# Layer 2 of a fused four-layer graph network: norm, turn and routing logits made tile by tile in the second pass

## The chip, the cores and the metric

The kernel runs on 1 core of one Trainium2 chip. The metric is the device time of one execution in microseconds (us), the median of the runs shown.

## What is computed

Four layers stand in a row. Each is a residual step with a graph operator (`gnn`) and a residual step with a feed-forward part (`ffn`), both behind a LayerNorm. There are 3125 nodes with 256 features in float32 and 50000 edges. The change lies where layer 2's graph operator ends and its mixture of experts begins:

```python
# x = x + L2_gnn(layernorm(x), edges, edge_weight, ...)
def _block(x, ei, ew, g, bln, W, b):
    return x + relu(gcn_conv(layer_norm(x, g, bln), ei, ew, W, b))
x = _block(x, ..., ln6_g, ln6_b, W6, b6)
x = _block(x, ..., ln7_g, ln7_b, W7, b7)
return x @ Wp.T + bp

# x = x + L2_ffn(layernorm(x), ...)
shared = relu(relu(x @ sW1 + sb1) @ sW2 + sb2) @ sW3 + sb3
gates = softmax(x @ gW + gb)                 # 4 experts
topv, topi = top_k(gates, 2); topw = softmax(topv)
return shared + sum over the two chosen experts of topw * expert(x)
```

## The kernel before

The nodes stand in T = 25 tiles of P = 125 rows. `X` (the residual) and `XN` (the normed input) lie in SBUF as 25 tiles of 125x256 and stay there from layer to layer. The work is a chain of stages: the context manager `stage` (L83) closes a stage by letting SyncE, ScalarE, TensorE and VectorE drain, add one to `phase_done` and wait until all four have. GpSimd isn't part of these and runs along.

**Layer 2's graph operator** (`layer2_gnn`, L1674). The weighted adjacency matrix lies in DRAM as 25 stripes (`weight_cells`). A pass over the graph takes the 25 stripes one after the other. For each, SyncE loads a block of 125x3125 into one of three buffers (L1716), and TensorE adds up 25 products 125x125 times 125x256 into one PSUM accumulator (L1752, "a block" below; each product is two matmul records in the trace, so 50). There are two passes, `p` = 0 and 1, hence blocks i = 0 to 49. Behind block j TensorE turns tile j-1 (two transposes, L1728) and multiplies tile j-2 by W7 or Wp (L1737), so a pass has T + 2 steps. ScalarE copies what was turned out of PSUM (L1776, L1779). VectorE makes `u` of a block (L1796, L1802); in pass 0 it also norms it (L1806 to L1814, with the root on ScalarE, L1767), in pass 1 it adds bp and the residual for tile j-2 (L1819, L1821). That last add makes the final X of the tile. Beside it all GpSimd scatters edge records for layer 3 (`sort.scatter`, L1669), paced by the blocks.

**Layer 2's mixture** (`layer2_ffn`, L2270) begins with four short stages. The first has SyncE issue 13 loads of the mixture's weights and biases (L2296 to L2301) and waits for none of them. The second is `gate` (L1969), a call of `linear` (L250) with a norm: VectorE takes statistics of all 25 tiles of X (L187) and small terms of all tiles at once (L190 to L204), then scales 13 tiles to `XN` (L208) while ScalarE scales 12 (L218). TensorE turns each tile (L316, two transposes) and two tiles later multiplies it by the 256x4 gate weights (L328), ScalarE copies what was turned (L351), and VectorE adds the bias and puts the logits away (L1972). The third stage is `route` (L1911: softmax, the two best, their weights), the fourth makes the coefficients (L2309, L2312). Then comes the main stage of the mixture: it first waits for the 13 loads, VectorE adds the shared bias sb3 to all of X at once (L2401), and TensorE runs the shared network and the four experts on `XN`, five tiles at a time (L2337, L2355, L2367), while VectorE adds the products to X (L2411, L2413).

Of the kernel before, what the change touches and what calls it, by code (L numbers as in the profile page):

```python
# [1673 lines left out]
def layer2_gnn(nc, g, a, sort):  # L1674
# [4 lines left out]
    with ExitStack() as ctx:  # L1679
# [13 lines left out]
        acc, psT, psL = ps("acc", [128, 3, 512]), ps("psT", [128, 2, 512]), ps("psL", [128, 2, 512])  # L1693
        loaded = [sem(f"loaded{j}") for j in range(BLOCKS)]
# [6 lines left out]
        def _(sp):  # L1701
# [19 lines left out]
        def _(pe):  # L1721
# [20 lines left out]
            for p in range(2):  # L1742
                if p == 1:
                    pe.wait_ge(made_read, T)
                for j in range(T + 2):
                    if j < T:
                        i = p * T + j
                        pe.wait_ge(loaded[i % BLOCKS], 16 * (i // BLOCKS + 1))
                        if i >= 3:
                            pe.wait_ge(acc_read, i - 2)  # L1750
                        for t in range(T):
                            last = nc.tensor.matmul(acc[0:P, i % 3, 0:D], blocks[0:P, i % BLOCKS, t * P:(t + 1) * P],  # L1752
                                                    H[p][0:P, t, :], start=(t == 0), stop=(t == T - 1))
                        last.then_inc(summed, 1)
                    if 1 <= j <= T:
                        turn(p, j - 1)
                    if 2 <= j:
                        multiply(p, j - 2)

        @block.scalar  # L1760
        def _(act):
            act.wait_ge(w_loaded, 16 * 7)
            for p in range(2):
                for j in range(T + 2):
# [16 lines left out]
                    if p == 0 and j >= 2:  # L1781
# [3 lines left out]
                                             scale=g.dinv2[0:P, m:m + 1]).then_inc(made_read, 1)  # L1785

        @block.vector
        def _(dve):
            dve.wait_ge(w_loaded, 16 * 7)
            for p in range(2):  # L1790
                for j in range(T + 2):
# [24 lines left out]
                    if p == 1 and j >= 2:  # L1816
# [5 lines left out]
                        dve.drain()  # L1822

# [145 lines left out]
def gate(nc, g, tag, w, b, n, out, more_loads=()):  # L1969
# [3 lines left out]
    linear(nc, g, tag, g.XN, D, w, b, n, put, norm_of=g.X, more_loads=more_loads)  # L1973

# [295 lines left out]
def layer2_ffn(nc, g, a):  # L2270
# [3 lines left out]
    with ExitStack() as ctx:  # L2274
        sb, ps, sem = bufs(nc, ctx, "f2")
        logits, chosen, weight = sb("logits", [128, T, NE]), sb("chosen", [128, T, 2]), sb("weight", [128, T, 2])
        hot, coef = sb("hot", [128, T, 2, NE]), sb("coef", [128, T, NE])
        s1, s2, s3 = sb("s1", [128, K2, 256]), sb("s2", [128, 2, 128]), sb("s3", [128, D])
        e1, e2, e3 = sb("e1", [128, K2, NE, H1]), sb("e2", [128, NE, H2]), sb("e3", [H2 + 1, NE, D])
        sb1_, sb2_, sb3_ = sb("sb1", [128, 2]), sb("sb2", [128, 1]), sb("sb3", [128, D])  # L2280
        eb1, eb2 = sb("eb1", [128, NE]), sb("eb2", [H2, NE])
        loaded = sem("loaded")

        with stage(nc, g) as block:
            @block.sync
            def _(sp):
                for out, src in ((s1[:, :, :], a["L2_ffn_sW1"].rearrange("(k p) n -> p k n", p=128)),
                                 (s2[:, :, :], a["L2_ffn_sW2"].rearrange("(k p) n -> p k n", p=128)),
                                 (s3[:, :], a["L2_ffn_sW3"]),
                                 (e1[:, 0], a["L2_ffn_eW1"][:, 0:128, :].rearrange("e p n -> p e n")),  # L2290
                                 (e1[:, 1], a["L2_ffn_eW1"][:, 128:256, :].rearrange("e p n -> p e n")),
                                 (e2[:, :, :], a["L2_ffn_eW2"].rearrange("e p n -> p e n")),
                                 (e3[0:H2], a["L2_ffn_eW3"].rearrange("e p n -> p e n")),
                                 (e3[H2:H2 + 1, :, :], a["L2_ffn_eb3"].rearrange("(a e) n -> a e n", a=1)),
                                 (sb3_[:, :], a["L2_ffn_sb3"].partition_broadcast(128))):
                    sp.dma_start(out, src).then_inc(loaded, 16)  # L2296
                with nc.allow_non_contiguous_dma("a few hundred values"):
                    sp.dma_start(sb1_[:, :], a["L2_ffn_sb1"].rearrange("(k p) -> p k", p=128)).then_inc(loaded, 16)
                    sp.dma_start(sb2_[:, :], a["L2_ffn_sb2"].rearrange("(p k) -> p k", k=1)).then_inc(loaded, 16)
                    sp.dma_start(eb1[:, :], a["L2_ffn_eb1"].rearrange("e p -> p e")).then_inc(loaded, 16)  # L2300
                    sp.dma_start(eb2[:, :], a["L2_ffn_eb2"].rearrange("e p -> p e")).then_inc(loaded, 16)  # L2301

        gate(nc, g, "f2g", a["L2_ffn_gW"], a["L2_ffn_gb"], NE, logits)
# [23 lines left out]
        def _(pe):  # L2327
            pe.wait_ge(loaded, 208)
# [43 lines left out]
        def _(act):  # L2372
            act.wait_ge(loaded, 208)
# [321 lines left out]
def build(nc, a, out):  # L2695
    with ExitStack() as ctx:
# [60 lines left out]
        with ExitStack() as sorted_edges:  # L2757
            g.slots = sorted_edges.enter_context(nc.sbuf_tensor("slots", [128, ST + R // 2, 4], F32))
            with ExitStack() as keep:
# [7 lines left out]
                layer2_gnn(nc, g, a, sort)  # L2767
                layer2_ffn(nc, g, a)
# [24 lines left out]
```

## Time and profile before

| | |
|---|---|
| median of 3 runs | 4196.51 us (4194.24 to 4197.27) |
| the profiled execution | 4226.76 us |
| its span | 4225.0 us |
| mean granted TensorE clock | 0.864 |
| TensorE busy | 3233.1 us (77%) |
| VectorE busy | 1454.5 us (34%) |
| ScalarE busy | 809.9 us (19%) |
| GpSimd busy | 2336.8 us (55%) |

Busy times and all rows are those of the one profiled execution. Times within it are us from the start of its span. "PEld" is TensorE's weight load, which overlaps its matmuls; "PEclk" is the TensorE clock that was granted, as a share of 2.4 GHz. "issue" stands for time in which an engine waited for nothing that the profile shows, "remote" for a release that the profile doesn't place on an engine.

### The profile page before, as it was taken

The page shows a single profiled execution, that of the slowest core. Times are in us where ns is not written, and L with a number is a line of the kernel's source. Part 1 is how long each engine was busy: PE and PEld are TensorE (multiplying, and loading weights), DVE is VectorE, ACT ScalarE, POOL GpSimd, SP SyncE. Part 2 cuts the span into 40 slices and gives each one's busy share as a digit, 9 for nine tenths or more (in the row PEclk, how much of TensorE's full clock was granted, in tenths as well). Part 3 has the DMA queues.
Part 4 walks back from the last instruction along what each step waited for, and adds up shares of the span by engine and source line. Part 5 has one row for each costly group of instructions (what it writes and reads, how often), then busy time and mean ns, then how long its engine had stood idle before and what let it go on. Part 6 is the DMA issues. An engine that isn't in the chain of part 4 may idle for free.

```text
span 4225.0 us, 52499 instructions
## 1 busy us (share of the span) xinstructions
PE 3233.1 (77%) x18065; PEld 2470.3 (58%) x18066; DVE 1454.5 (34%) x3546; ACT 809.9 (19%) x2103; POOL 2336.8 (55%) x1876
## 2 busy tenths in 40 slices
PE   0899965485999997699189999969879555555698
PEld 0555553364999997588178878855534333333565
DVE  3333345623461113311721111133343343444344
ACT  0666631211000001133221000013310000001111
POOL 5587888887666666566646656510000666664121
PEclk9999986777999997699599999979989666776799
DMA  8664222124999997487434333400034433335432
GB/s 335 244 187 111 5 6 6 1 18 88 297 282 285 260 264 181 111 227 228 88 132 137 125 123 123 138 16 0 0 126 139 138 92 91 94 91 126 124 114 78
DMA packets 345581, 552.26 MB, mean 131 GB/s; under 512 B 175479, under 2 KB 221473, under 8 KB 328435
## 3 DMA queue, kind: packets, MB, share of 16 engines
q1 hardware_dynamic: 180208, 377.11, 27.8%
q0 software_dynamic: 161552, 132.29, 16.3%
q10 hardware_dynamic: 3600, 40.00, 2.3%
q8 instruction: 128, 2.10, 0.2%
q14 instruction: 93, 0.76, 0.1%
HBM read 410.96 MB, written 137.73 MB: 130 GB/s over the span
## 4 chain that ended last, share of the span: by engine, by line
PE 52%; POOL 19%; issue 13%; DMA 5%; DVE 4%; ACT 1%; ACTq 1%; SPq 1%; another core or an unknown queue 1%; DVEq 1%; POOLq 0%; PEldq 0%
POOL count_cells L465 15%; PE g_acc L1752 13%; PE g_acc L1438 13%; PE g3g_pp L942 5%; PE g_psO L1878 4%; POOL g3g_got L929 3%; PE f3e_pH L2636 3%; PE f_pR L2355 3%; PE f3e_pY L2645 2%; DMA count_cells<-cells_count,added_row 1%; PE f1e_pH L2166 1%; PE f1e_pY L2188 1%; DMA g3g_got<-relations,g3g_idx 1%; POOL weight_cells L882 1%
## 5 line engine op out<-in xcount | busy, mean ns | idle before, releaser
L882 POOL DMA_INDIRECT weight_cells<-added_weight,added_row x391 | 632.0, 1616 | 286.5 <-DMA weight_cells<-added_weight,added_row 158.4
L929 POOL DMA_INDIRECT g3g_got<-relations,g3g_idx x416 | 402.4, 967 | 699.9 <-ACTq L95 509.7
L465 POOL DMA_INDIRECT count_cells<-cells_count,added_row x391 | 651.6, 1666 | 209.6 <-issue 118.6
L1438 PE MATMUL g_acc<-XN,g_blocks 125*125 125x128 f32 x5000 | 565.0, 274 | 42.4 <-DMA g_blocks<-count_cells 40.0
L1752 PE MATMUL g_acc<-g_H,g_blocks 125*125 125x256 f32 x2500 | 562.4, 383 | 30.9 <-issue 16.1
L1438 PEld LDWEIGHTS g_acc<-XN,g_blocks 125*125 125x125 f32 x5000 | 556.8, 189 | 47.1 <-issue 40.2
L942 PE MATMUL g3g_pp<-g3g_got,g3g_hot 128*125 128x256 f32 x832 | 333.1, 543 | 275.0 <-issue 205.2
L1752 PEld LDWEIGHTS g_acc<-g_H,g_blocks 125*125 125x125 f32 x2500 | 473.8, 190 | 112.5 <-issue 40.8
L1669 POOL DMA_INDIRECT slots_dram<-sort_rec,sort_row x392 | 379.5, 968 | 274.2 <-issue 110.2
L942 PEld LDWEIGHTS g3g_pp<-g3g_got,g3g_hot 128*125 128x125 f32 x832 | 192.9, 259 | 415.3 <-issue 234.6
L968 DVE TENSOR_TENSOR X<-X,g3g_pp 125x256 f32 x416 | 175.3, 421 | 347.3 <-DMA edges_other<-digits_dram 179.8
L735 ACT ACTIVATE same_same<-same_scores 128x128 bf16<-128x128 f32 (+7 forms) x392 | 255.1, 651 | 145.4 <-PE same_scores L724 127.9
L720 PE MATMUL same_scores<-edges_other,edges_own 11*128 11x512 bf16 (+2 forms) x490 | 206.9, 483 | 22.5 <-ACT same_same L735 22.5
L1796 DVE SCALAR_TENSOR_TENSOR g_tmp<-g_acc,dinv,g_b 125x256 f32<-125x256 f32 x50 | 24.2, 484 | 517.0 <-PE g_acc L1752 334.9
L1878 PE MATMUL g_psO<-g_w,g_xT 128*125 128x512 f32 x400 | 174.5, 597 | 0.0
L1459 ACT ACTIVATE g_uT<-g_psT 128x125 f32<-128x125 f32 (+1 forms) x75 | 20.6, 275 | 612.0 <-PE g_psT L1413 475.8
L2613 POOL DMA_INDIRECT out_x<-f3e_ys,f_to x32 | 31.2, 976 | 189.9 <-DVE f3e_ys L2691 189.9
L2166 PEld LDWEIGHTS f1e_pH<-f1e_xT,f1e_w 128*128 128x128 f32 x1040 | 125.9, 194 | 16.6 <-ACT f1e_xT L2197 8.7
L2166 PE MATMUL f1e_pH<-f1e_xT,f1e_w 128*128 128x128 f32 x1040 | 130.2, 279 | 6.6 <-ACT f1e_xT L2197 4.4
L1878 PEld LDWEIGHTS g_psO<-g_w,g_xT 128*125 128x125 f32 x400 | 75.6, 190 | 95.3 <-issue 95.1
L722 PE MATMUL same_scores<-edges_other,edges_own 11*128 11x128 bf16 x392 | 119.9, 306 | 7.7 <-DMA edges_other<-digits_dram 7.7
L2188 PE MATMUL f1e_pY<-w,f1e_hT 128*128 x512 | 122.0, 381 | 0.0
(647 smaller groups left out, 4713.0 us busy)
## 6 DMA issues: line engine op xcount, KB each, us to landing
g_blocks<-count_cells SPq DMA_DIRECT2D x500, 312.5 KB
g_blocks<-weight_cells SPq DMA_DIRECT2D x50, 1562.5 KB
count_cells<-edges_stripe ACTq DMA_DIRECT2D x25, 1562.5 KB
weight_cells<-edges_stripe POOLq DMA_DIRECT2D x25, 1562.5 KB
f1e_w<-in_L_ffn_w SPq DMA_DIRECT2D x68, 512.0 KB
relations<-g_ys SPq DMA_DIRECT2D x25, 896.0 KB
f_w<-in_L_ffn_w SPq DMA_DIRECT2D x16, 1024.0 KB
f1e_b<-in_L_ffn_b SPq DMA_DIRECT2D x68, 128.0 KB
```

Of the source, the lines that this page charges most:

```text
L465: pool.indirect_dma_start(out=rows, out_offset=bass.IndirectOffsetOnAxis(ap=g.cell_row[:, t:t + 1], axis=0), in_=g.cell_count[:, t:t + 1], ...
L720: nc.tensor.matmul(self.scores[:, k % self.SCORES, lo:hi], own[:, j, n:n + 128], other[:, j, lo:hi], start=True, stop=True)
L735: self.nc.scalar.activation(self.same[:, k % self.SAME, 0:n], self.scores[:, k % self.SCORES, 0:n], ACT.Relu, accum_out=self.found[:, k:k ...
L882: pool.indirect_dma_start(out=rows, out_offset=bass.IndirectOffsetOnAxis(ap=g.cell_row[:, t:t + 1], axis=0), in_=g.cell_weight[:, t:t + 1] ...
L929: pool.indirect_dma_start(out=got[:, j, :], out_offset=None, in_=table[:, :], in_offset=bass.IndirectOffsetOnAxis(ap=idx[:, n:n + 1], axis ...
L942: last = nc.tensor.matmul(pp[0:P, n // 2 % BANKS, half], hot[:, j, :], got[:, j, :], start=True, stop=True)
L968: last = nc.vector.tensor_tensor(part, part, pp[0:P, n // 2 % BANKS, half], ALU.add)
L1438: last = nc.tensor.matmul(acc[0:P, i % ACCS, 0:128], blocks[0:P, i % BLOCKS, t * P:(t + 1) * P], rhs[p][:, t, :], start=(t == 0), stop=(t ...
L1669: pool.indirect_dma_start(out=g.slots_dram[:, :], out_offset=bass.IndirectOffsetOnAxis(ap=self.row[:, c:c + 1], axis=0), in_=self.rec[:, c ...
L1752: last = nc.tensor.matmul(acc[0:P, i % 3, 0:D], blocks[0:P, i % BLOCKS, t * P:(t + 1) * P], H[p][0:P, t, :], start=(t == 0), stop=(t == T ...
L1878: last = nc.tensor.matmul(psO[0:P, c, :], xT[:, j, k, :], w[:, k, 2 * c:2 * c + 2, :].rearrange("p r n -> p (r n)"), start=(k == 0), stop= ...
L2166: last = nc.tensor.matmul(pH[:, j % 2, f * 128:(f + 1) * 128], w1[:, j % AHEAD, k, f * 128:(f + 1) * 128], xT[:, j % 2, k * 128:(k + 1) * ...
```

## The change

The stages of loads and of the gate are taken out of `layer2_ffn`. What they did is done in pass 1 of `layer2_gnn`, by two new classes.

`TileGate` holds the gate's work for one tile: `norm` (VectorE: statistics, a small sum, then the scaling to `XN`), `root` (ScalarE), `turn` (TensorE, two transposes into a PSUM bank of its own), `copy` (ScalarE), `multiply` (TensorE, four columns into the same bank) and `put` (VectorE). There is one buffer of each, and the turn of tile t waits for the norm of t and for the put of t-1. In step j of pass 1, VectorE norms tile j-2 as soon as its X is done, and puts tile j-3; TensorE turns tile j-3 in the middle of block j and multiplies it at the end of the step. The pass gets one step more, T + 3.

`SharedExperts` holds the mixture's weights. SyncE issues the gate's two loads and the 13 loads of the mixture just ahead of the load of block 25, that is of pass 1's first. Behind the norm of a tile VectorE adds the shared bias sb3 to that tile of X; the add over all of X in the main stage goes, as do that stage's three waits for the loads.

```diff
@@ layer2_gnn, SyncE @@
                 if i == 0:
                     sp.wait_ge(g.weights_added, 16 * (EC + 1))
+                if i == T:
+                    gating.load(sp)
+                    loads.load(sp)
@@ TensorE @@
-                for j in range(T + 2):
+                for j in range(T + 2 + p):
                     if j < T:
...
                         for t in range(T):
+                            if p == 1 and t == T // 2 and j >= 3:
+                                gating.turn(pe, j - 3)
                             last = nc.tensor.matmul(acc[0:P, i % 3, 0:D], blocks[0:P, i % BLOCKS, t * P:(t + 1) * P],
...
                     if 1 <= j <= T:
                         turn(p, j - 1)
-                    if 2 <= j:
+                    if 2 <= j < T + 2:
                         multiply(p, j - 2)
+                    if p == 1 and j >= 3:
+                        if j >= T:
+                            gating.turn(pe, j - 3)
+                        gating.multiply(pe, j - 3)
@@ ScalarE @@
+                    if p == 1 and j >= 3:
+                        gating.copy(act, j - 3)
...
+                    if p == 1 and 2 <= j < T + 2:
+                        gating.root(act, j - 2)
@@ VectorE @@
                         nc.vector.tensor_tensor(g.X[0:P, j - 2, :], tmp2[0:P, :], g.X[0:P, j - 2, :], ALU.add)
                         dve.drain()
+                        gating.norm(dve, j - 2)
+                        if j == 2:
+                            dve.wait_ge(loads.loaded, 208)
+                        nc.vector.tensor_tensor(g.X[0:P, j - 2, :], g.X[0:P, j - 2, :], loads.sb3[0:P, :], ALU.add)
+                    if p == 1 and j >= 3:
+                        gating.put(dve, j - 3)
@@ class TileGate @@
+    def norm(self, dve, t):
+        nc, x = self.nc, self.g.X[0:P, t, :]
+        nc.vector.bn_stats(self.st[0:P, :], x)
+        dve.drain()
+        nc.vector.bn_aggr(self.mv[0:P, :], self.st[0:P, :])
+        dve.drain()
+        nc.vector.tensor_scalar(self.ve[0:P, :], self.mv[0:P, 1:2], EPS, None, ALU.add).then_inc(self.var_ready, 1)
+        dve.wait_ge(self.std_ready, t + 1)
+        nc.vector.reciprocal(self.rstd[0:P, :], self.std[0:P, :])
+        dve.drain()
+        nc.vector.tensor_scalar(self.g.XN[0:P, t, :], x, self.mv[0:P, 0:1], self.rstd[0:P, :],
+                                ALU.subtract, ALU.mult).then_inc(self.normed, 1)
+    def turn(self, pe, t):
+        pe.wait_ge(self.normed, t + 1)
+        if t:
+            pe.wait_ge(self.put_away, t)
+        for k in range(K2):
+            last = nc.tensor.transpose(self.bank[:, k * P:(k + 1) * P], g.XN[0:P, t, k * 128:(k + 1) * 128], g.ident[0:P, 0:P])
+        last.then_inc(self.turned, 1)
+    def copy(self, act, t):
+        act.wait_ge(self.turned, t + 1)
+        if t:
+            act.wait_ge(self.made, t)
+        self.nc.scalar.copy(self.xT[:, :, :], self.bank[:, 0:K2 * P]...).then_inc(self.turn_read, 1)
+    def multiply(self, pe, t):
+        pe.wait_ge(self.turn_read, t + 1)
+        if t == 0:
+            pe.wait_ge(self.loaded, 32)
+        for k in range(K2):
+            last = self.nc.tensor.matmul(self.bank[0:P, 256:256 + self.n], self.xT[:, k, :], self.w[:, k, :], ...)
+        last.then_inc(self.made, 1)
@@ layer2_ffn @@
-        gate(nc, g, "f2g", a["L2_ffn_gW"], a["L2_ffn_gb"], NE, logits)
...
-            pe.wait_ge(loaded, 208)
...
-            act.wait_ge(loaded, 208)
...
-            dve.wait_ge(loaded, 208)
-            nc.vector.tensor_tensor(g.X[0:P], g.X[0:P], wide(sb3_[0:P, :], P, T, D), ALU.add)
```

TensorE at the end of pass 1 and at the start of the gate, before (`g_acc` is a block, `g_psT` and `g_psL` the pass's own turn and multiply, `f2g_psT` and `f2g_psO` the gate's; an f32 matmul here is two records in the trace):

```order
L1752 MATMUL g_acc<-g_H,g_blocks 125x256 x25
L1728 MATMUL g_psT<-ident,g_u 128x125 x2
L1737 MATMUL g_psL<-g_wp,g_uT 125x256 x2
L1728 MATMUL g_psT<-ident,g_u 128x125 x2
L1737 MATMUL g_psL<-g_wp,g_uT 125x256 x4
L99 UNCONDITIONAL_BRANCH x2
L304 UNCONDITIONAL_BRANCH
L316 MATMUL f2g_psT<-ident,XN 128x125 x6
L328 MATMUL f2g_psO<-f2g_w,f2g_xT 125x4 x2
```

The same place now, from the last block on (`g_gate` is the gate's bank: `g_gate<-ident,XN` a turn, `g_gate<-f2g_w,f2g_xT` a multiply):

```order
L1758 MATMUL g_acc<-g_H,g_blocks 125x256 x12
L2038 MATMUL g_gate<-ident,XN 128x125 x2
L1758 MATMUL g_acc<-g_H,g_blocks 125x256 x13
L1732 MATMUL g_psT<-ident,g_u 128x125 x2
L1741 MATMUL g_psL<-g_wp,g_uT 125x256 x2
L2052 MATMUL g_gate<-f2g_w,f2g_xT 125x4 x2
L1732 MATMUL g_psT<-ident,g_u 128x125 x2
L1741 MATMUL g_psL<-g_wp,g_uT 125x256 x2
L2038 MATMUL g_gate<-ident,XN 128x125 x2
L2052 MATMUL g_gate<-f2g_w,f2g_xT 125x4 x2
L1741 MATMUL g_psL<-g_wp,g_uT 125x256 x2
```

Each of blocks 28 to 49 is now split by a turn of the gate, and a multiply of the gate follows each step; behind the last block three tiles of the gate are left, where there were 25.

VectorE in one step of pass 1 now; before, only the first four rows stood there:

```order
L1810 SCALAR_TENSOR_TENSOR g_tmp<-g_acc,dinv,g_b 125x256
L1816 SCALAR_TENSOR_TENSOR g_u<-g_tmp,XN 125x256
L1833 TENSOR_TENSOR g_tmp<-g_psL,g_bp 125x256
L1835 TENSOR_TENSOR X<-g_tmp,X 125x256
L2017 BN_STATS f2g_st<-X 125x6
L2019 BN_AGGR f2g_mv<-f2g_st 125x2
L2021 TENSOR_SCALAR f2g_ve<-f2g_mv 125x1
L2023 RECIPROCAL f2g_rstd<-f2g_std 125x1
L2025 TENSOR_SCALAR XN<-X,f2g_mv,f2g_rstd 125x256
L1840 TENSOR_TENSOR X<-X,f_sb 125x256
L2060 TENSOR_TENSOR f2g_logits<-g_gate,f2g_bias 125x4
```

The last seven rows are new in the step: the norm of the tile whose X was just made, the shared bias, and the put of the tile before it.

## Rows read from the trace of the kernel before

**Rows 1.** The page, the chain that ended last by engine.
```profile
PE 52%; POOL 19%; issue 13%; DMA 5%; DVE 4%; ACT 1%; ACTq 1%; SPq 1%; another core or an unknown queue 1%; DVEq 1%; POOLq 0%; PEldq 0%
```
**Rows 2.** Windows: length, busy us (count) by engine, clock, DMA share, GB/s.
```profile
2467.45:2785.68 318.23, 306.30 (x1386) 259.30 (x1387) 40.55 (x92) 9.88 (x46) 181.63 (x188) 0.98 0.33 113
2785.68:2839.38 53.70, 32.46 (x166) 31.21 (x164) 21.24 (x80) 16.03 (x42) 0.00 (x0) 0.57 0.13 31
```
**Rows 3.** Chain of waits: a clean block, then behind pass 1 (start, us, what).
```profile
2623.41 10.79 PE g_acc L1752 x50
2634.20 0.21 PE g_psT L1728 x2
...
2788.62 0.42 DVE X L1821
...
2789.64 0.43 DVE X L1821
...
2790.32 0.38 SPq L2296
...
2799.21 4.67 DVE f2g_st L187 x14
...
2809.93 1.51 PE f2g_psT L316 x6
2811.44 0.69 PE f2g_psO L328 x4
...
2836.86 2.33 PE f2g_psO L328 x12
2839.22 0.16 DVE f_logits L1972
```
**Rows 4.** Timeline: a clean block of pass 1, and the pass's end.
```profile
2623.24 2.97 PE L1752 MATMUL g_acc<-g_H,g_blocks 125*125 125x256 f32 x13
2623.48 0.42 DVE L1819 TENSOR_TENSOR g_tmp<-g_psL,g_bp 125x256 f32<-125x256 f32 x1
2624.00 0.42 DVE L1821 TENSOR_TENSOR X<-g_tmp,X 125x256 f32<-125x256 f32 x1
...
2787.32 0.42 DVE L1821 TENSOR_TENSOR X<-g_tmp,X 125x256 f32<-125x256 f32 x1
```
**Rows 5.** Timeline: first and last operation of one tile's norm in pass 0.
```profile
2175.03 0.43 DVE L1806 BATCH_NORM_STATS2 g_st<-XN 125x6 f32<-125x256 f32 x1
...
2176.46 0.41 DVE L1814 TENSOR_SCALAR g_u<-XN,g_mv,g_rstd 125x256 f32<-125x256 f32 x1
```
**Rows 6.** Windows of layer 1's table and of the gate, and groups of the first.
```profile
984.00:998.00 14.00, 14.00 (x129) 13.93 (x128) 7.80 (x24) 10.46 (x29) 11.59 (x8) 1.00 0.24 2
2811.10:2836.80 25.70, 25.70 (x136) 25.68 (x134) 6.02 (x31) 13.52 (x34) 0.00 (x0) 0.50 0.00 1
...
L316 PE MATMUL g1a_psT<-ident,XN 125*128 125x125 f32 x42 | 8.0, 272 | 0.0
```
**Rows 7.** Timeline at two late blocks, and who VectorE waited for in pass 1.
```profile
2574.74 10.96 PE L1752 MATMUL g_acc<-g_H,g_blocks 125*125 125x256 f32 x50
2580.95 0.42 DVE L1821 TENSOR_TENSOR X<-g_tmp,X 125x256 f32<-125x256 f32 x1
...
2598.49 3.83 PE L1752 MATMUL g_acc<-g_H,g_blocks 125*125 125x256 f32 x17
2603.27 0.42 DVE L1821 TENSOR_TENSOR X<-g_tmp,X 125x256 f32<-125x256 f32 x1
...
DVE g_tmp L1796 <- PE g_acc L1752: 162.0, 17, 18.1
```
**Rows 8.** Window in which block 25 is loaded.
```profile
2430.70:2437.00 6.30, 6.30 (x32) 5.49 (x31) 2.25 (x7) 1.26 (x4) 4.49 (x5) 1.00 0.76 258
```
**Rows 9.** Timeline: the shared bias, and VectorE's first product in the mixture.
```profile
2850.11 6.83 DVE L2401 TENSOR_TENSOR X<-X,f_sb 125x6400 f32<-125x6400 f32 x1
2870.05 0.42 DVE L2411 TENSOR_TENSOR f_acc<-f_pO,X 125x256 f32<-125x256 f32 x1 [13.11 <-PE f_pO L2367]
```

More of the change, by code:

```diff
@@ L1763, in _ @@
             for p in range(2):
-                for j in range(T + 2):
+                for j in range(T + 2 + p):
+                    if p == 1 and j >= 3:
+                        gating.copy(act, j - 3)
                     if p == 0 and j < T:
@@ L1790, in _ @@
             for p in range(2):
-                for j in range(T + 2):
+                for j in range(T + 2 + p):
                     if j < T:
@@ L2267, in _, with __init__, load, layer2_ffn @@
                         norm.tile_act(t)
-def layer2_ffn(nc, g, a):
+class SharedExperts:
+    def __init__(self, nc, g, a, ctx):
+        NE, _, H1 = a["L2_ffn_eW1"].shape
+        H2 = a["L2_ffn_eW2"].shape[2]
+        sb, ps, sem = bufs(nc, ctx, "f2")
+        self.nc, self.a = nc, a
+        self.s1, self.s2, self.s3 = sb("s1", [128, K2, 256]), sb("s2", [128, 2, 128]), sb("s3", [128, D])
+        self.e1, self.e2, self.e3 = sb("e1", [128, K2, NE, H1]), sb("e2", [128, NE, H2]), sb("e3", [H2 + 1, NE, D])
+        self.sb1, self.sb2, self.sb3 = sb("sb1", [128, 2]), sb("sb2", [128, 1]), sb("sb3", [128, D])
+        self.eb1, self.eb2 = sb("eb1", [128, NE]), sb("eb2", [H2, NE])
+        self.H2 = H2
+        self.loaded = sem("loaded")
+    def load(self, sp):
+        nc, a, H2, loaded = self.nc, self.a, self.H2, self.loaded
+        for out, src in ((self.s1[:, :, :], a["L2_ffn_sW1"].rearrange("(k p) n -> p k n", p=128)),
+                         (self.s2[:, :, :], a["L2_ffn_sW2"].rearrange("(k p) n -> p k n", p=128)),
+                         (self.s3[:, :], a["L2_ffn_sW3"]),
+                         (self.e1[:, 0], a["L2_ffn_eW1"][:, 0:128, :].rearrange("e p n -> p e n")),
+                         (self.e1[:, 1], a["L2_ffn_eW1"][:, 128:256, :].rearrange("e p n -> p e n")),
+                         (self.e2[:, :, :], a["L2_ffn_eW2"].rearrange("e p n -> p e n")),
+                         (self.e3[0:H2], a["L2_ffn_eW3"].rearrange("e p n -> p e n")),
+                         (self.e3[H2:H2 + 1, :, :], a["L2_ffn_eb3"].rearrange("(a e) n -> a e n", a=1)),
+                         (self.sb3[:, :], a["L2_ffn_sb3"].partition_broadcast(128))):
+            sp.dma_start(out, src).then_inc(loaded, 16)
+        with nc.allow_non_contiguous_dma("a few hundred values"):
+            sp.dma_start(self.sb1[:, :], a["L2_ffn_sb1"].rearrange("(k p) -> p k", p=128)).then_inc(loaded, 16)
+            sp.dma_start(self.sb2[:, :], a["L2_ffn_sb2"].rearrange("(p k) -> p k", k=1)).then_inc(loaded, 16)
+            sp.dma_start(self.eb1[:, :], a["L2_ffn_eb1"].rearrange("e p -> p e")).then_inc(loaded, 16)
+            sp.dma_start(self.eb2[:, :], a["L2_ffn_eb2"].rearrange("e p -> p e")).then_inc(loaded, 16)
+def layer2_ffn(nc, g, a, gating, loads):
     NE, _, H1 = a["L2_ffn_eW1"].shape
@@ L2280, in layer2_ffn @@
[L2280 to L2301, printed above, removed]
```

46 lines of the change are left out of this document (38 added, 8 removed).

## The prediction

> **What bounds the kernel now.** I read the page first. The chain that ended last is over half TensorE's [rows 1]. Then the windows of the stretch that the change touches. The second pass of layer 2 runs from 2467.45 to 2785.68 us with TensorE busy for 306.30 of 318.23 us at a clock of 0.98, while VectorE is busy for 40.55 us and ScalarE for 9.88. The stretch from the end of its last block to the last logit takes 53.70 us [rows 2]. So inside the pass each microsecond added to TensorE costs one, and work of VectorE and ScalarE is free as long as TensorE doesn't wait for it; behind the pass everything stands on the chain.
>
> The chain of waits says what those 53.70 us are: the last X is done at 2790.07, SyncE issues fifteen loads until VectorE may begin the statistics at 2799.21, the first tile is turned at 2809.93, TensorE turns and multiplies 25 tiles until 2839.19, and the last logit is done at 2839.38 [rows 3]. Over those 25 tiles the granted clock is 0.50, that is 1.2 of 2.4 GHz [rows 6].
>
> **What goes.** Two stages (loads, gate) and all that stands in them: what is left of the 53.70 us is the new tail.
>
> **The new tail.** VectorE sets it. When the last block ends, three tiles are left. Tile 22's two adds (of bp, and to X) stand where they did and end at 2787.74 [rows 4]; such a pair takes 1.02 us, from 2788.62 to 2789.64 [rows 3]. Behind it now comes the norm. Its price is a row of pass 1, which does the same steps: from the statistics at 2175.03 to the end of the scaling at 2176.87 is 1.84 us [rows 5], 1.92 with the gap ahead. Then the shared bias, an add of 125x256 like the two of a pair, 0.52 with its gap (2623.48 to 2624.00) [rows 4], and the put of the tile before, 0.22 (0.16 in [rows 3] and a gap). So tile 22 is done at 2787.7 + 2.7 = 2790.4, and tiles 23 and 24 follow at 1.02 + 2.66 = 3.68 us each: 2797.7. TensorE's turns and multiplies of 22 and 23 fit between. After the last norm the last tile must still be turned, copied, multiplied and put; in the old gate stage the first tiles took from 2809.93 to 2811.44 + 0.69 = 2812.13 at the low clock [rows 3], 2.2 us, and the put 0.16: 2800.1. The tail is 2800.1 - 2785.7 = 14.4 us in place of 53.7, **39.3 us less**. Routing follows as before.
>
> **What TensorE takes on inside the pass.** Of the 25 tiles, 22 are turned and 21 multiplied ahead of the last block's end; I charge 22. A tile brings two transposes and four matmul records of four columns, each with a weight load: six pairs. In a clean block the two transposes of the pass's own turn cost 0.21 us at the full clock, at 2634.20 [rows 3]. A pair with 128 columns cost 14.00 / 129 = 0.109 us at a clock of 1.00 in layer 1's table, and the same six pairs as here cost 25.70 / 136 = 0.189 us each at 0.50 [rows 6]. I take 0.109 (an estimate: 0.189 halved would be 0.095): 6 x 0.109 = 0.65 us, 22 x 0.65 = **14.3 us more**. Bounds: the narrow matmuls free, 22 x 0.21 = 4.6; all at the low clock's price, 22 x 1.13 = 24.9.
>
> **What TensorE may wait for.** The turn of tile j-3 stands 24 matmul records into block j (24 of 50 records that take 10.79 us [rows 3], 5.2 us) and waits for the norm and for the put behind it. In a clean block the pass's X is done at 2624.42, the norm, the shared bias and the put take 1.92 + 0.52 + 0.22 = 2.66 us more, 2627.08, and TensorE comes to the turn at 2623.24 + 5.2 = 2628.4 [rows 4, 5]: **slack 1.4 us**, no wait. What stands behind the turn on TensorE is the other half of the block, so a miss costs its full length. Three blocks of the pass show a miss to come: there VectorE sees the block's end some 3 us late. In the first X ends at 2581.37, with 2.66 us more at 2584.03, while TensorE began the next block at 2574.74 and comes to the turn at 2579.94: it would wait 4.1 us. In the second it is 2603.69 + 2.66 against 2598.49 + 5.2, so 2.7 us; the third, near 2718, is like the first: 10.9 us in all [rows 7]. The profiled execution is 30 us above the median, so some of this lateness may belong to the profiling; I take half, **5.4 us**, and keep 0 and 10.9 as bounds.
>
> **Edits at nothing.** ScalarE's 25 copies and 25 roots: in the old gate stage it was busy for 13.52 us with the copies and half of the scalings [rows 6], and in the pass it is idle for 97% of 318 us [rows 2]; were it late, the multiply at the block's end, 6 us behind the copy, would wait. SyncE issues the fifteen loads ahead of block 25's: that delays this transfer by some 9 us of issue (2790.32 to 2799.21 [rows 3]) and some 6 us of moving their 1.7 MB (31 GB/s over 53.70 us [rows 2]) at the 258 GB/s of a block's load. Block 25's load moved from 2430.7 to 2437.0 [rows 8], and TensorE used it from 2467.45 [rows 2]; 30 us of slack cover 15. The next block's load waits for a later sum anyway. The wide bias add of 6.83 us in the mixture's stage goes, and it was hidden: VectorE waited 13.11 us for its first product after it [rows 9]. GpSimd's scatter is paced by the blocks, not by this.
>
> **The sum.** -39.3 + 14.3 + 5.4 = -19.6 us. The profiled execution took 4226.8 us (span 4225.0), 30.3 above the median of the runs, and should come to 4207.2, span 4205.4; taken from the median of 4196.5 it is **4176.9 us**.
>
> One thing speaks against this change. The granted clock is 1.00 in clean blocks of the passes [rows 8], though each has two transposes; but it was 0.50 through the whole old gate stage, although TensorE was never idle there [rows 6]. The Trainium skill, "TensorE: Matmul & The Clock Gate", Part 4, says that transposes don't count as TensorE being busy, and that page's part on oscillation warns of short pauses between bursts. By that rule, if the new turns and waits lowered the clock, the time would come out as in rival 2 and not as in the sum; layer 1's table argues against it, since it stood at 1.00 with 42 of 129 matmul records transposes [rows 6]. So the trace agrees only in part.
>
> **Rivals.**
> 1. *The pass gives most of it back.* Narrow pairs at the low clock's price and every late block paid in full: -39.3 + 24.9 + 10.9 = -3.5, 4193.0 us. For it: the one row with four-column matmuls has that price. Against: that row's clock. Chance 0.09.
> 2. *The clock falls inside the pass.* A block's 50 records take 10.79 us at the full clock [rows 3]; at half they take twice that. 22 blocks give 237 us more, 4414 us; it decides against the change from two blocks on. Chance 0.02.
> 3. *VectorE late in every block.* The wait for the norm in the middle of a block replaces the gate stage. With 25.0 us in hand (39.3 - 14.3) and 1.4 us of slack, it turns the sign once VectorE is 25.0 / 22 + 1.4 = 2.5 us later in every block. At the 4.1 us lost in the worst block it is 90 - 25 = 65 us: 4262 us, slower. For it: VectorE gets eleven operations for four, and the slack is small. Against: in 17 blocks of the pass VectorE's first instruction was released by TensorE's block on time [rows 7]. Chance 0.03.
> 4. *It doesn't do what it says:* the loads delay block 25, or routing waits for something else that the gate stage had hidden. At most the 9.1 us of the load stage (2790.07 to 2799.21) come back, 4186 us; nothing in the windows points there. Chance 0.04.
>
> The forecast has 0.82. In it nearly all is faster by more than 8.4 us, 0.2%, which is about what a measurement of this kernel can tell from no change. Rival 4 too is faster; rival 1 is within 0.2%; 2 and 3 are slower. Faster 0.86, same 0.09, slower 0.05. The range runs from the best bounds, -39.3 + 4.6 = -34.7 (4161.8), to rival 1's, a little inside both: 4162 to 4192.
>
> **What the changed profile should show.** The second pass some 20 us longer (338), blocks of 12.5 us instead of 11.87; from the end of the last block to the last logit 14 us; routing starting some 20 us earlier; the old gate stage's lines gone; the granted clock in the pass still near 0.98. Waits of TensorE's new transposes for the scaling on VectorE should be few, and where VectorE sees a block's end late. Many of them, or a clock under 0.9 in the pass, would make the prediction wrong; so would a tail over 25 us.

## The result, and the profile after

| | before | after |
|---|---|---|
| median of 8 runs each | 4195.38 us (4185.87 to 4213.36) | 4173.91 us (4162.06 to 4182.66) |
| ratio, 95% interval | | 0.9944 (0.9930 to 0.9958) |
| the profiled execution, its span | 4226.76, 4225.0 us | 4177.88, 4176.1 us |
| mean granted TensorE clock | 0.864 | 0.874 |

The change is faster by 0.56%, about 23.5 us at the ratio (17.6 to 29.4 over the interval); 19.6 was forecast. The profiled pair lies 48.9 us apart, over twice as much, so it alone can't be read as the effect.

The page of the changed kernel: busy time by engine, and the chain that ended last by engine (before: [rows 1]).

```profile
PE 3210.9 (77%) x18065; PEld 2452.1 (59%) x18066; DVE 1474.7 (35%) x3648; ACT 808.1 (19%) x2115; POOL 2328.0 (56%) x1876
...
PE 51%; POOL 21%; issue 12%; DMA 5%; DVE 5%; ACTq 1%; another core or an unknown queue 1%; ACT 1%; SPq 1%; DVEq 1%; POOLq 0%; PEldq 0%
```

The windows of pass 1 and of what follows it, in the columns of [rows 2].

```profile
2459.00:2782.00 323.00, 316.55 (x1521) 273.19 (x1522) 78.79 (x245) 24.37 (x95) 185.42 (x193) 0.98 0.34 114
2782.00:2798.00 16.00, 8.95 (x40) 6.48 (x38) 9.35 (x33) 4.04 (x12) 0.00 (x0) 0.70 0.00 1
```

VectorE has 245 records in the pass where it had 92, TensorE is busy for 98% of it, and the clock is 0.98 in both kernels. The old stretch of 53.70 us is gone; what follows the pass has 40 TensorE records instead of 166.

The chain of waits of the changed kernel: one clean step of the pass, then the last wait in the pass and the tail (start, us, what).

```profile
2504.06 0.21 PE g_gate L2038 x2
2504.27 5.61 PE g_acc L1758 x26
2509.88 0.21 PE g_psT L1732 x2
2510.10 0.86 PE g_psL L1741 x4
2510.96 0.33 PE g_gate L2052 x4
2511.30 5.28 PE g_acc L1758 x24
...
2523.49 0.33 PE g_gate L2052 x4
...
2782.39 0.21 PE g_psT L1732 x2
...
2792.81 0.41 DVE XN L2025
...
2793.77 0.66 PE g_gate L2038 x2
2794.46 0.38 ACT f2g_xT L2045
2794.88 1.02 PE g_gate L2052 x4
2795.92 0.16 DVE f2g_logits L2060
```

A step is now 12.52 us (2510.96 + 0.33 to 2523.49 + 0.33); before it was 10.79 + 0.21 and the 0.87 of the pass's multiply. The 0.65 us more are the new turn, 0.21, the new multiply, 0.33, and 0.10 in the block itself, whose two parts take 5.28 + 5.61 = 10.89. The last block's end is seen by VectorE at 2782.43 and the last logit is done at 2796.08: a tail of 13.65 us for 53.70.

One step of the pass in the timeline of the changed kernel shows the slack (operation, shapes, and in brackets the idle time before).

```profile
2661.84 0.42 DVE L1835 TENSOR_TENSOR X<-g_tmp,X 125x256 f32<-125x256 f32 x1
...
2663.76 0.41 DVE L2025 TENSOR_SCALAR XN<-X,f2g_mv,f2g_rstd 125x256 f32<-125x256 f32 x1
2664.09 0.42 DVE L1840 TENSOR_TENSOR X<-X,f_sb 125x256 f32<-125x256 f32 x1
2664.42 0.15 DVE L2060 TENSOR_TENSOR f2g_logits<-g_gate,f2g_bias 125x4 f32<-125x4 f32 x1
2666.70 0.38 PE L2038 MATMUL g_gate<-ident,XN 125*128 125x125 f32 x2
```

The put ends at 2664.57 and the turn starts at 2666.70: 2.1 us of slack, where 1.4 were forecast. And the waits of TensorE in the changed kernel's pass (who waited for whom: us in total, times, longest).

```profile
PE g_gate L2038 <- DVE f2g_logits L2060: 5.9, 2, 3.0
```

Only two turns waited, for the put. The timeline of the second one shows why.

```profile
2764.90 0.38 PE L1732 MATMUL g_psT<-ident,g_u 125*128 125x125 f32 x2
...
2770.26 0.48 DVE L1810 SCALAR_TENSOR_TENSOR g_tmp<-g_acc,dinv,g_b 125x256 f32<-125x256 f32 x1 [13.30 <-remote]
2770.30 0.43 ACT L1791 COPY g_uT<-g_psT 128x125 f32<-128x125 f32 x2 [8.91 <-remote]
...
2774.78 0.65 PE L2038 MATMUL g_gate<-ident,XN 125*128 125x125 f32 x2 [3.02 <-DVE f2g_logits L2060]
```

TensorE had ended the block and begun the next turn at 2764.90, yet VectorE's first instruction behind it starts at 2770.26, 5.4 us later, where it is 0.20 in a clean step (2782.23 and 2782.43 at the pass's end). Everything behind it comes late, the put too. VectorE had been idle for 13.30 us, so it is not the added work that made it late, and ScalarE's copy of the turned tile (the turn ends at 2765.28) starts only at 2770.30 as well. What held both up is not shown. The other one, at 2719.79, has the same start: 2710.09 and 2712.85.

### The profile page after: what moved, and what is told of

Same layout as the page of the kernel before. It is cut to its first block, busy times and chain, and to the rows that moved or that the text cites. A ratio compares the mean times of both kernels' runs of the same rounds, so it can differ in the third digit from the quotient of the medians.

```text
span 4176.1 us, 52647 instructions
## 1 busy us (share of the span) xinstructions
PE 3210.9 (77%) x18065; PEld 2452.1 (59%) x18066; DVE 1474.7 (35%) x3648; ACT 808.1 (19%) x2115; POOL 2328.0 (56%) x1876
## 4 chain that ended last, share of the span: by engine, by line
PE 51%; POOL 21%; issue 12%; DMA 5%; DVE 5%; ACTq 1%; another core or an unknown queue 1%; ACT 1%; SPq 1%; DVEq 1%; POOLq 0%; PEldq 0%
POOL count_cells L465 15%; PE g_acc L1438 13%; PE g_acc L1758 12%; POOL g3g_got L929 5%; PE g_psO L1898 4%; PE g3g_pp L942 3%; PE f3e_pH L2732 3%; PE f2m_pR L2454 3%; PE f3e_pY L2741 2%; PE f1e_pH L2254 2%; PE f1e_pY L2276 2%; DMA count_cells<-cells_count,added_row 2%; POOL weight_cells L882 1%; DMA count_cells<-edges_stripe 1%
## 5 line engine op out<-in xcount | busy, mean ns | idle before, releaser
L1438 PE MATMUL g_acc<-XN,g_blocks 125*125 125x128 f32 x5000 | 564.9, 274 | 39.3 <-DMA g_blocks<-count_cells 36.9
L1810 DVE SCALAR_TENSOR_TENSOR g_tmp<-g_acc,dinv,g_b 125x256 f32<-125x256 f32 x50 | 24.2, 484 | 477.4 <-PE g_acc L1758 259.9
L2254 PEld LDWEIGHTS f1e_pH<-f1e_xT,f1e_w 128*128 128x128 f32 x1040 | 125.7, 194 | 12.5 <-ACT f1e_xT L2285 5.2
```

What stands on the lines that cost most here:

```text
L1438: last = nc.tensor.matmul(acc[0:P, i % ACCS, 0:128], blocks[0:P, i % BLOCKS, t * P:(t + 1) * P], rhs[p][:, t, :], start=(t == 0), stop=(t ...
L2254: last = nc.tensor.matmul(pH[:, j % 2, f * 128:(f + 1) * 128], w1[:, j % AHEAD, k, f * 128:(f + 1) * 128], xT[:, j % 2, k * 128:(k + 1) * ...
```

## Experiments

They ran in three batches, on chips that the record numbers 3 (loads moved, turn at 20 and at 3, multiply twice), 5 (changed again, the two with the wide bias add, 128 columns beside) and 10 (before again, the two delays, TensorE warmed up). For the pair above the record names no chip. The kernel before took 4117.7, 4116.7 and 4113.9 us in the three batches, where it took 4195 in the pair above. So it and the changed one were also run again, each with a trace, and the other traces are compared with these two. Each ratio is against the kernel before in the same batch. None leaves work out; some add work whose result is not used.

| kernel | median us | ratio (95%) | pass | tail | main | rest |
|---|---|---|---|---|---|---|
| before, again | 4115.47 | 1.0003 (0.9991 to 1.0015) | 300.1 | 53.80 | 208.9 | 1100.2 |
| changed, again | 4083.24 | 0.9920 (0.9905 to 0.9935) | 314.0 | 14.05 | 202.8 | 1100.5 |
| loads moved alone | 4107.66 | 0.9979 (0.9969 to 0.9988) | 300.1 | 44.92 | 209.6 | 1100.8 |
| turn at product 20 | 4085.45 | 0.9931 (0.9919 to 0.9943) | 314.0 | 14.05 | 202.7 | 1099.8 |
| turn at product 3 | 4131.97 | 1.0034 (1.0021 to 1.0047) | 358.7 | 14.04 | 202.8 | 1100.2 |
| multiply twice | 4095.80 | 0.9947 (0.9933 to 0.9962) | 323.2 | 15.23 | 202.6 | 1099.2 |
| wide bias add back | 4088.64 | 0.9930 (0.9915 to 0.9945) | 314.0 | 13.38 | 207.0 | 1102.8 |
| wide bias, turn at 20 | 4089.34 | 0.9932 (0.9915 to 0.9949) | 314.1 | 13.27 | 204.3 | 1102.1 |
| 128 columns beside, in old gate | 4134.02 | 1.0044 (1.0030 to 1.0058) | 300.1 | 75.08 | 209.7 | 1099.8 |
| main stage 1.4 us later | 4089.15 | 0.9939 (0.9920 to 0.9958) | 314.0 | 14.01 | 202.3 | 1099.2 |
| main stage 2.7 us later | 4088.82 | 0.9941 (0.9921 to 0.9961) | 314.0 | 14.05 | 204.4 | 1096.2 |
| TensorE warmed up | 4087.73 | 0.9930 (0.9909 to 0.9950) | 317.0 | 14.05 | 204.9 | 1099.4 |

The last four columns are read from each kernel's one trace: "pass" from VectorE's first instruction behind block 24 to that behind block 49, "tail" from there to the last logit done, "main" from TensorE's first turn in the mixture's main stage to the start of VectorE's last add of a product to the running sum `acc`, "rest" what follows. Routing and coefficients between tail and main take 11.15 us before and 11.32 after.

### The two kernels again

> The kernel before, profiled beside the next ones. If the stalls and late blocks of the first pair belong to the chip and not to the kernel: 25 blocks of 11.87 us in pass 1, 53.7 us from the last block's end to the last logit, and the mixture's main stage at 203 to 210 us from its first turn to its last product. Rival (they are the kernel's): again some 20 us of stalls in pass 1.

> The changed kernel itself, beside the next ones on the same chip. My sum: 20 us less than before, 0.995. Rival (the 49 us of the profiled pair are the change's own): 0.990 or less.

The changed kernel comes to 0.9920 of the time before, a larger gain than the expected 0.995, and a smaller one than the rival's 0.990. Two kernels that differ from the changed one by almost nothing (the turn at product 20, the first delay) have 0.9931 and 0.9939. So the gain in these batches is some 25 to 33 us.

In both traces every block of pass 1 is clean, which makes them the best reading of the change, though they are of two batches. From the kernel before to the changed one the pass takes 13.9 us more, the tail 39.75 less, routing 0.2 more, the main stage 6.1 less, the rest 0.3 more, and the pass starts 0.8 earlier; together 32.4, the difference of the spans (4114.6 and 4082.2), and close to that of the medians. The windows of the pass show neither kernel idle nor at a low clock, first before, then changed:

```profile
2454.00:2740.00 286.00, 286.00 (x1350) 248.16 (x1349) 40.71 (x92) 9.91 (x46) 180.33 (x187) 1.00 0.37 125
```

```profile
2453.00:2753.00 300.00, 300.00 (x1478) 261.20 (x1478) 79.08 (x245) 22.46 (x90) 182.82 (x189) 1.00 0.36 120
```

So the lateness of VectorE's view of a block, on which the prediction put 5.4 us, is in neither trace. That speaks for the expectation's first reading, that the kernel doesn't cause it. Whether the chip does is not shown.

### The loads alone

In the kernel before, the 13 loads of the mixture's weights go ahead of block 25's, and their stage goes; the gate stays as it was.

```diff
+                if i == T:
+                    loads.load(sp)
@@ layer2_ffn @@
-        with stage(nc, g) as block:
-            @block.sync
-            ...
```

> The kernel before, with the 13 loads of the mixture issued ahead of block 25's load, and the load stage gone. My sum (the tail is worth 39.3 us, of which the load stage is 9.1, and the loads cost nothing in pass 1): 9 us less than the kernel before, the last X to the first statistics 0.2 us in place of 9.1, no wait of TensorE for block 25. Rival (the loads delay block 25 or cost TensorE something in the pass): no change or slower, with a wait of TensorE for g_blocks at the start of pass 1.

The tail falls from 53.80 to 44.92 us and the pass stays at 300.1: the load stage was worth 8.9 us, and the loads in their new place cost nothing. The chain of waits of this kernel behind the pass shows what is left between the last X and the statistics:

```profile
2746.65 0.42 DVE X L1823
...
2747.45 4.67 DVE f2g_st L187 x14
```

From the end of the last X at 2747.08 it is 0.4 us, where it was 9.1 [rows 3]. Of the tail's 39.75 us, 8.9 are the loads', the other 30.9 the gate's.

### Where the turn stands

```diff
-                            if p == 1 and t == T // 2 and j >= 3:
+                            if p == 1 and t == 20 and j >= 3:
```

> The changed kernel with the gate's turn behind the 20th of a block's 25 products instead of the 12th: TensorE comes to it 3.5 us later and has 5.6 us of slack in place of 2.1. My theory (TensorE waits for VectorE in a few blocks only, 5.9 us in the profiled execution): no wait for the gate's turn inside the pass, clean blocks 12.52 us as in the changed kernel, the same tail, 2 to 6 us less. Rival (the split of a block itself costs, by filling and emptying the array, and the waits are a by-product): no change, blocks a little longer or shorter.

Pass and tail are those of the changed kernel, and the 2 to 6 us that were expected didn't come. With no wait in the pass there is nothing to win by a later turn. Whether it would save the 5.9 us of the first pair wasn't tried.

The other way, three products into the block (`t == 3`):

> The changed kernel with the gate's turn behind the 3rd product instead of the 12th: TensorE comes to it 3.9 us earlier, which takes the 2.1 us of slack and 1.8 us more. My theory (the slack in the block decides, every microsecond of lateness costs TensorE one, 22 times): a clean block 14.3 us in place of 12.5, 22 x 1.8 = 39 us more than the changed kernel, so slower than before by about 15 us. Rival (the slack is larger than I count, since VectorE overlaps the steps, or TensorE catches up later in the block): under 15 us more than the changed kernel, still faster than before.

This is rival 3 made to happen, and it is slower than the kernel before. TensorE's waits in this kernel from 2460 to 2770 us, and then one of them in its chain:

```profile
PE g_gate L2038 <- DVE f2g_logits L2060: 33.6, 19, 1.8
```

```profile
2656.41 0.21 PE g_psT L1732 x2
...
2660.00 0.41 DVE XN L2025
2660.41 0.33 DVE X L1840
2660.74 0.08 DVE f2g_logits L2060
2660.83 0.14 issue
2660.96 0.41 PE g_gate L2038 x2
2661.37 9.50 PE g_acc L1758 x44
2670.87 0.21 PE g_psT L1732 x2
```

The step is 14.46 us (2656.41 to 2670.87), 1.94 more than 12.52. The wait is 1.75 of that. The rest is the turn behind it, which takes 0.41 us on the chain after a wait and 0.21 in a stream. The amount of work is the same, and 22 steps of this kind turn a gain of 33 us into a loss of 14 (22 x 1.94 is 43), as the expectation had it. The clock of this pass was 0.99: it fell once, to 0.50 for 3.4 us from 2543.5, and that step took 16.20 us. In the passes of the later pair it didn't fall. One fall in 22 pauses of 1.8 us doesn't show that a pause caused it; it does show that 21 of them did not lower the clock.

### The price of the narrow pairs

The gate's multiply is issued twice, the first time into columns that nobody reads.

```diff
         for k in range(K2):
+            self.nc.tensor.matmul(self.bank[0:P, 384:384 + self.n], self.xT[:, k, :], self.w[:, k, :], ...)
+        for k in range(K2):
             last = self.nc.tensor.matmul(self.bank[0:P, 256:256 + self.n], ...)
```

> The changed kernel with each of the gate's multiplies done twice (the first time into spare columns of the bank). My theory (a pair of weight load and four-column matmul costs 0.08 to 0.11 us at the full clock and doesn't lower it): blocks 12.52 + 4 x 0.09 to 0.11 = 12.9 to 13.0 us, 8 to 10 us more than the changed kernel, the clock in the pass 0.98. Rival (narrow work lowers the clock): a clock under 0.9 in the pass and tens of microseconds more.

The chain of this kernel, the end of a step (L2052 is the added multiply):

```profile
2650.79 0.87 PE g_psL L1741 x4
2651.66 0.33 PE g_gate L2052 x4
2651.99 0.44 PE g_gate L2055 x4
```

The first four pairs cost 0.33 us (0.083 each), the next four 0.44 (0.110 each). The pass is 9.2 us longer, 0.44 in each of the 21 steps with a multiply ahead of the last block's end, and its clock is 1.00. So a pair with four columns costs 0.083 to 0.110 us at the full clock, and the 0.109 taken for it lies at the upper end of that.

### The wide bias add put back

The add of sb3 tile by tile goes, the add over all of X in the main stage returns.

```diff
-                        nc.vector.tensor_tensor(g.X[0:P, j - 2, :], g.X[0:P, j - 2, :], loads.sb3[0:P, :], ALU.add)
...
+            nc.vector.tensor_tensor(g.X[0:P], g.X[0:P], wide(loads.sb3[0:P, :], P, T, D), ALU.add)
```

> The changed kernel with the shared bias added to all of X at once in the mixture's main stage again, as before. My theory (that add was hidden under TensorE's first group of tiles, and the three adds of tiles 22 to 24 lie on the tail at 0.33 to 0.5 us each): the main stage's first product as early as in the changed kernel, slack 0.4 us larger, tail 1 us shorter, so 1 to 3 us less. Rival (the wide add of 6.8 us delays the main stage's start): up to 7 us more.

> The changed kernel with both: the gate's turn behind the 20th product, and the shared bias added at once in the main stage. My theory: the gains of the two add up, 3 to 8 us less than the changed kernel, no waits for the gate's turn in the pass, tail 12.6 us. Rival (stalls that TensorE has anyway take up the waits): the same as the changed kernel.

The tail is 0.7 us shorter, for VectorE has one add less per tile there. The time isn't: the main stage is 1.6 to 4.2 us longer in these traces, and the rest about 2. The expected 1 to 8 us less didn't come; the medians are 5.4 and 6.1 us above the changed kernel's in the same batch. The intervals of the ratios overlap, so it is a hint, not shown, that moving the bias brought a few microseconds.

### The clock of the gate stage

In the kernel before, each tile's multiply in the gate gets two more products of 128 columns, whose result is not used.

```diff
+                        if tag == "f2g":
+                            nc.tensor.matmul(psO[0:P, m % BANKS, 128:256], xT[0:kc[k], m % PLACES, k, :], g.ident[:, :], ...)
```

> The kernel before; in layer 2's gate TensorE makes two more matmuls of 128 columns per tile (with the identity, into spare columns) ahead of the two of 4 columns. If narrow matmuls are why the granted clock stays at 0.50 there: it rises to 1.00 within the stage, and the 25 tiles, with 10 pairs for 6, take 25 x 10 x 0.109 = 27 us, about the 29 us of before, so no change in time in spite of two thirds more work. Rival (the clock stays at half for another reason, such as the pauses of the stage before): 25 x 10 x 0.19 = 48 us, 19 us more.

The windows of this kernel's gate, and its groups on TensorE there (operation, shapes, count, busy us and mean ns, idle before):

```profile
2765.00:2812.00 47.00, 47.00 (x235) 47.00 (x235) 5.52 (x30) 13.10 (x33) 0.00 (x0) 0.50 0.00 0
```

```profile
L329 PE MATMUL f2g_psO<-ident,f2g_xT 128*125 128x128 f32 x95 | 25.6, 420 | 0.0
L332 PE MATMUL f2g_psO<-f2g_w,f2g_xT 128*125 128x4 f32 x96 | 20.2, 316 | 0.0
L316 PE MATMUL f2g_psT<-ident,XN 125*128 125x125 f32 x44 | 14.5, 432 | 0.0
```

TensorE was never idle for 47 us, transposes were 44 of 235 records, and the clock stayed at 0.50, 1.2 of 2.4 GHz. The tail grew by 21.3 us, 0.213 for each of the 100 added pairs, twice the 0.109 of a pair with 128 columns at 1.00 [rows 6]. So the share of transposes alone doesn't say which clock a stretch gets: 42 of 129 stood at 1.00 in layer 1's table, 44 of 235 at 0.50 here. The time came out as the expectation's rival had it. Why the gate's clock stays at 0.50 is open: 96 of the records still have four columns, and what went before the stage was not changed.

### The main stage, moved and warmed up

The changed kernel's main stage was 6.1 us shorter, which no step of the change explains. Two kernels let it begin later, by repeats of the last small add of the coefficients (4, then 8). The third issues products of 256 columns that nobody reads ahead of it: ten in routing, two in the coefficients' stage, two right before its first turn.

```diff
+                for _ in range(4):
+                    dve.drain()
+                    nc.vector.tensor_tensor(coef[0:P], hot[0:P, :, 0, :], hot[0:P, :, 1, :], ALU.add)
```

> The changed kernel with four repeats of the last small sum before the mixture's main stage, 4 x 0.34 = 1.4 us of delay, nothing else. My theory (the main stage's length hangs on when within its groups the clock falls, so on where the stage begins, not on the shared bias): a main stage that differs by 1 us or more from the changed kernel's 203.4, with falls of the clock at other places. Rival (the 6.8 us between the two kinds come from the wide add of the shared bias): 203.4 us again, and 1.4 us more in all.

> The same with eight repeats, 2.7 us of delay. My theory: a third length of the main stage, between 203 and 210 us, so a total that is not simply 2.7 us more. Rival: 203.4 us and 2.7 us more.

> The changed kernel; TensorE makes 14 matmuls of 256 columns for nothing while routing and the first copies run (ten in routing, two in the coefficients' stage, two ahead of the main stage's first turn). My theory: TensorE is idle there in any case, and the clock stands at 1.00 when the main stage begins, where the changed kernel has 0.50 for 7.5 us: 3 to 4 us less in the first 10 us of the main stage, besides what the later falls of the clock give or take (0 to 6 us). Rival (the clock falls again in the 3 us until the first turn, or the matmuls outlast routing): no gain, or 1 to 2 us more.

The windows of the whole main stage, of the kernel before and of the changed one:

```profile
2805.48:3014.38 208.90, 187.89 (x660) 116.26 (x660) 64.46 (x124) 72.11 (x155) 0.00 (x0) 0.93 0.00 0
```

```profile
2778.93:2981.73 202.80, 182.00 (x660) 112.52 (x660) 58.05 (x124) 72.21 (x156) 0.00 (x0) 0.96 0.00 0
```

The same 660 matmuls take 5.9 us less at a clock of 0.96 than at 0.93. With the stage cut into windows of 2 us, 1 minus the clock, times 2 us, adds up to 14.8 us for the kernel before, 8.6 for the changed one, 8.1 and 10.7 for the two delays, 11.1 for the warm-up, 13.8 and 10.8 for the two with the wide add. The stage's length less this sum is 193.2 to 194.2 us in all of them. So the 6.1 us are time at the low clock that didn't occur. What decides how much of it occurs is not settled. The second delay gave a third length, 204.4, as expected; the first gave 202.3, within 0.5 us of the changed kernel's 202.8, where 1 us or more was expected.

The warm-up didn't get hold of it. The first 8 us of the main stage, changed kernel and warmed up, then a later stretch of the latter, and its last warm-up products:

```profile
2778.93:2786.93 8.00, 7.19 (x19) 4.14 (x20) 0.00 (x0) 2.43 (x7) 0.00 (x0) 0.56 0.00 0
```

```profile
2786.76:2794.76 8.00, 7.04 (x26) 4.37 (x25) 0.00 (x0) 3.47 (x8) 0.00 (x0) 0.89 0.00 0
2808.76:2814.76 6.00, 5.84 (x14) 4.62 (x15) 3.92 (x9) 0.00 (x0) 0.00 (x0) 0.52 0.00 0
```

```profile
2784.99 1.97 PE L2406 MATMUL f2m_pR<-f_s,ident 128*128 128x256 f32 x4 [1.96 <-DVE f2m_h2e L2513]
```

It did keep the clock up at the start, 0.89 for 0.56, and the clock fell 22 us later instead. The last two products also stand on the chain ahead of the first turn: from the last logit to that turn it takes 13.1 us in place of 11.3. No gain was left.

## Why the prediction was right

The time, 4173.91 us, is 3.0 below the 4176.9 forecast and inside the range. The two large terms were right for the reason given. That the sum came so near is luck in part: the term for waits was a guess on a miscounted row, and a shorter main stage had no term. Step by step ("the first pair" is that of the result, "the later pair" the two kernels run again):

- **The tail, -39.3 us.** Measured -40.05 (53.70 to 13.65) in the first pair, -39.75 (53.80 to 14.05) in the later one. The price of a norm taken from pass 0 and the pace set by VectorE were right. A tile costs VectorE 3.24 us of work there, not 3.68, because the shared bias and the put start 0.33 us after the operation ahead of them, not a full 0.42 and a gap. The last tile's turn, copy, multiply and put took 2.86 us from the end of its norm at 2793.22, not 2.4.
- **TensorE inside the pass, +14.3 us.** Measured +13.9 between the two clean passes, 0.65 us a step as worked out, with one multiply fewer than the 22 charged. That it was six pairs at 0.109 is right as a sum only: the two transposes took 0.21, the four narrow pairs 0.33, and 0.1 came in the block that the turn splits.
- **Waits for VectorE, +5.4 us.** The weakest step, near the first pair's number by luck. There two turns waited for 5.9 us together, each where VectorE saw a block late, as in [rows 7]. In the later pair there was no late block and no wait. The prediction also miscounted: it found three late blocks and a bound of 10.9 us, and the same trace has two more. The chain of waits at the first of them, and the add that makes X (timeline):

```profile
2635.28 4.85 PE g_acc L1752 x22
2640.13 0.73 issue
2640.86 0.38 PE g_acc L1752
...
2641.57 0.69 PE g_acc L1752 x2
```

```profile
2644.98 0.47 DVE L1821 TENSOR_TENSOR X<-g_tmp,X 125x256 f32<-125x256 f32 x1
```

With 2.66 us more, X ending at 2645.45 would let the turn start at 2648.11, while TensorE begins the block's 25th record at 2641.9: a wait of 6.2 us. In the other, X ends at 2763.01 and the 25th record starts at 2759.19: 6.5 us. By the prediction's own method the bound is some 23.6 us and not 10.9, and half of it 11.8, by which the forecast would have been 4183. TensorE has pauses of its own in these two blocks, which might have hidden part of such a wait. The slack, worked out as 1.4 us, is 2.1: the new multiply delays TensorE by 0.33 us ahead of the block, and the shared bias and the put overlap more.

- **Edits at nothing.** Right: the loads alone left the pass at 300.1 us, ScalarE's copies never held up a multiply in the pass, and routing and coefficients took 11.3 us for 11.1.
- **The wide bias add at nothing.** Right in the sum, but the main stage was not unchanged: it got shorter by 6.1 us, all of it time at the low clock, in the later pair and by 4.7 in the first (209.3 to 204.6). The prediction had no term for it. In the later pair it makes most of the difference between 25.8 us, the two terms above, and the 32.4 by which the spans differ. Its cause stays open. The four traces with the wide add on kernels of the old form have 208.9 to 209.7 us, the two with it on the changed kernel 204.3 and 207.0, the eight without it 202.3 to 204.9. That hints at the wide add, yet a shift of the start by some 1.4 us, from the first delay to the second, goes with 2.1 us, and each point is one execution.
- **The rivals.** Rival 1 needed the narrow pairs at the low clock's price; they had the full clock's. Rival 2 needed a fall of the clock in the pass that lasts; it was 0.98 and 1.00, with two more transposes in every step. The Trainium skill, "TensorE: Matmul & The Clock Gate", Part 4, says that transposes don't count as TensorE being busy in the way that other products do; by that rule the pass should have been nearer to a fall than before, and the trace doesn't show it. Rival 3's mechanism is real: with the turn nine products earlier (18 records at 10.79 / 50, 3.9 us, less the slack of 2.1, is a wait of 1.8) the change is slower than no change. A late step costs its wait and 0.2 us more. The gain of 33.5 us over 22 steps is 1.5 a step, so by this estimate the sign turns once VectorE is 2.1 + 1.3 = 3.4 us late in every step, or 3.0 with the first pair's gain of 23.5; 2.5 was forecast. Rival 4 is out: block 25 was not delayed.

Of the signs, the step of 12.5 us, the tail of 14, the clock in the pass and the few waits came as forecast. The pass was to be 20 us longer and routing to start 20 us earlier; in the profiled pair the pass took 326.5 us for 326.0, and routing started 43.3 us earlier (2796.08 for 2839.38), since the kernel before lost more in its pass than the changed one.

Why the profiled pair shows 48.9 us: in the kernel before, the pass took 25.9 us more than its clean form (326.0 against 300.1), in the changed one 12.5 (326.5 against 314.0). Of the 25.9 us, 11.4 are low clock (22.7 us of the pass at 0.50, where the clean passes have none), and the other 14.5 are about the 15.6 for which TensorE was idle, in pieces of "issue" between single records of a block, as in the lines above, which the clean blocks don't have. Of the 12.5, 6.8 are low clock, and the other 5.7 are about the 5.9 us of waits. Less the 13.4 us between them, the pair lies 35.5 apart, near the later pair's 32.4. Where these stalls come from wasn't tried, for no later trace of either kernel has them.

## What to carry to other kernels

A short stage that runs on data which an earlier loop finishes piece by piece can be folded into that loop, if the loop's bound engine takes on little (here 0.65 us a step) and the others are idle. What is saved is the stage's barrier, its ramp and its low clock, and it can be priced beforehand from rows of similar steps. Where a term is read from odd steps of a single trace, go through every step with the same test: here two of five late blocks were overlooked, and another execution had none. Place the new instruction on the bound engine where its input is done by a margin: half a block behind was safe by 2.1 us in clean steps, an eighth of a block behind cost more than the whole change brought. Compare stage by stage between traces without stalls before an effect of 0.5% is put down to the change.

## What the runs showed of the hardware

- With the turn at product 3, a wait cost TensorE more than its length: the turn behind it took 0.41 us on the chain against 0.21 in a stream.
- A pair of a weight load and a product with four columns cost 0.083 to 0.110 us at a granted clock of 1.00. At 0.50 a pair with 128 columns cost 0.213.
- The clock's falls come and go between executions. Right behind the short pause between the two passes, the first 100 records of pass 1 took 21.85 us in eleven of the fourteen traces, 24.1 and 24.2 in the first pair's, and 24.20 in that of the warmed-up kernel, whose work there is that of the changed one. The windows of the 6 us after the pause, changed (again) and warmed up:

```profile
2446.00:2452.00 6.00, 6.00 (x30) 5.22 (x29) 0.00 (x0) 0.00 (x0) 3.67 (x5) 1.00 0.03 4
```

```profile
2449.00:2455.00 6.00, 5.75 (x16) 4.61 (x17) 0.00 (x0) 0.19 (x1) 3.30 (x4) 0.58 0.03 4
```

- That accounts for 2.4 of the 3.0 us by which the warmed-up kernel's pass is longer (317.0). Differences of 2 to 3 us between single traces can be such a fall and nothing of the kernel.
- The same kernel took 4195 us in the first pair and 4114 to 4118 on the three chips of the later batches. The two profiled executions lie 110.4 us apart, 25.9 of it in this one pass and 65.1 behind the mixture's main stage. Whether the chip makes the difference is not shown.
